# Carried states and decayed C of a chunked scan as 16-bit halves, and three steps in other places

## What is computed

```python
scores = jnp.einsum('bclhn,bcshn->bchls', Cc, Bc) * Lmat      # Lmat = exp of differences of cs, lower triangle
Ydiag = jnp.einsum('bchls,bcshp->bclhp', scores, xdt)         # xdt = x * dt
states = jnp.einsum('bclhn,bchl,bclhp->bchpn', Bc, decay_states, xdt)
def step(carry, inp):
    st, cd = inp
    return carry * cd[:, :, None, None] + st, carry
...
Yoff = jnp.einsum('bclhn,bchpn,bchl->bclhp', Cc, prev, jnp.exp(cs))
Y = (Ydiag + Yoff) + x * D
```

## Time and profile before

| | us |
|---|---|
| runs before: median of 3 (lowest to highest) | 2434.76 (2432.14 to 2435.37) |
| profiled execution, its own time | 2433.26 |
| its span, first to last instruction | 2431.4 |
| PE busy (share of span) | 2343.2 (96%) |
| DVE busy | 1794.1 (74%) |
| ACT busy | 1584.3 (65%) |
| POOL busy | 1377.3 (57%) |

### The profile page before, as it was taken

The page is one execution under the profiler, slowest core; times in us unless marked ns, Lnnn a source line. Parts: engine busy times, 40 slices in busy tenths (PEclk is TensorE's granted clock), DMA queues, the critical chain, the costliest instruction groups (busy, mean ns, idle before and its releaser), DMA issues. The chain is left out here.

```text
span 2431.4 us, 49850 instructions
## 1 busy us (share of the span) xinstructions
PE 2343.2 (96%) x16008; PEld 1328.4 (55%) x16008; DVE 1794.1 (74%) x3250; ACT 1584.3 (65%) x3327; POOL 1377.3 (57%) x1178
## 2 busy tenths in 40 slices
PE   6999999999999999999999998879999999999898
PEld 3555555555555555555555554445555556555444
DVE  6777777777777787777777885567787777888613
ACT  6776776776776776776776774355665555655533
POOL 5576576576576576576576579344344434454323
PEclk8999999999999999999999999889999999999999
DMA  7343343343343343343343441320010110100000
GB/s 244 120 134 113 111 136 113 112 137 111 111 137 111 110 136 113 112 137 111 112 137 110 132 152 36 129 89 14 36 40 14 41 36 14 40 10 14 1 1 35
DMA packets 117294, 218.95 MB, mean 90 GB/s; under 512 B 10016, under 2 KB 43424, under 8 KB 115840
## 3 DMA queue, kind: packets, MB, share of 16 engines
q1 hardware_dynamic: 116992, 215.29, 27.0%
HBM read 212.10 MB, written 3.15 MB: 89 GB/s over the span
## 5 line engine op out<-in xcount | busy, mean ns | idle before, releaser
L990 ACT ACTIVATE E<-wq,cst 128x128 f32<-128x128 f32 x1024 | 311.7, 389 | 2.2 <-PEq L298 2.2
L256 DVE SCALAR_TENSOR_TENSOR xc<-bank,taps,xc 128x511 f32<-128x511 f32 (+2 forms) x384 | 283.0, 737 | 24.6 <-ACT xc L243 24.1
L1963 POOL TENSOR_TENSOR qT<-qT,qrot 128x512 f32<-128x512 f32 x64 | 81.3, 1270 | 358.3 <-DVE qrot L1852 358.3
L1297 POOL TENSOR_TENSOR acc<-acc,sq 128x512 f32<-128x512 f32 x112 | 162.6, 1452 | 183.5 <-ACT sq L1002 183.5
L61 PE MATMUL bank<-xhi,wx 128*128 128x512 f16 x640 | 242.7, 379 | 0.0
L60 PE MATMUL bank<-xlo,wx 128*128 128x512 f16 x640 | 242.6, 379 | 0.0
L59 PE MATMUL bank<-xhi,wx 128*128 128x512 f16 x640 | 242.5, 379 | 0.0
L1109 DVE TENSOR_TENSOR E<-E,cbm 128x1024 f32<-128x1024 f32 x128 | 235.0, 1836 | 0.9
L1280 POOL TENSOR_TENSOR ecs<-ecs,xcC 128x768 f32<-128x768 f32 x128 | 235.2, 1837 | 0.4 <-POOLq L298 0.4
L1176 DVE SCALAR_TENSOR_TENSOR u<-xc,D,bank 128x512 f32<-128x512 f32 x128 | 95.7, 747 | 177.1 <-PE bank L815 166.4
L1285 POOL TENSOR_TENSOR xw<-xt,wdec 128x384 f32<-128x384 f32 x128 | 106.5, 832 | 174.5 <-DVE xt L1128 174.4
(11 more groups left out here) (265 smaller groups left out, 6617.3 us busy)
## 6 DMA issues: line engine op xcount, KB each, us to landing
wq<-cs_rows SPq DMA_DIRECT2D x128, 512.0 KB, 4.0
ecs<-ecs_rows SPq DMA_DIRECT2D x128, 384.0 KB, 3.6
wx<-in_w_xbc SPq DMA_DIRECT2D x80, 256.0 KB, 2.6
wz<-in_w_z SPq DMA_DIRECT2D x64, 256.0 KB, 2.6
wo<-in_w_o SPq DMA_DIRECT2D x64, 256.0 KB, 3.9
wq<-in_wq SPq DMA_DIRECT2D x8, 1024.0 KB, 5.6
awo_raw<-in_wo SPq DMA_DIRECT2D x32, 256.0 KB, 3.0
wkv<-in_wkv SPq DMA_DIRECT2D x8, 512.0 KB, 3.7
```

Source lines behind the costliest of these rows:

```text
L256: self.nc.vector.scalar_tensor_tensor(out=dst[:, d:T], in0=self.k.bank[bank][:, 0:T - d], scalar=self.taps[:, bass.ds(g, 1), b, j, 3 - d:4 ...
L990: ins = nc.scalar.activation(E[t.i % 4][:, h, c], sc.csr[t.i % 2][:, h, c * P:(c + 1) * P], ACT.Relu, scale=-1.0, bias=head(sc.cst, t, c, h))
L1297: nc.gpsimd.tensor_tensor(acc[t.b][:], acc[t.b][:], sq[:], ALU.add).then_inc(acc_done, 1)
```

## The change

- The carried states are kept once (`st`, no longer two buffers). ACT casts them to f16 (`sthi`, `leading_states`), DVE subtracts this from them into f16 (`stlo`, `rest_of_states`). POOL makes beside `ecs` a remainder `ecslo` of it in f16, once the scan of the tile before is done (y_ready), since there is one buffer.
- The scan's fp32 product of state and C becomes three 16-bit ones per head and chunk, on the same 64-column halves. The scan waits for `cs_lo` and `st_lo` instead of cs_done.
- On DVE `xt` goes behind the first tap, `ylo` behind the second. On POOL `decayed_x` goes ahead of the low halves of the z weights.
- `exps` of two tiles are written at the end of odd slots instead of at the head of even ones.

```diff
@@ buffers
-        st = [sb(f"st{i}", [P, CH - 1, P]) for i in range(2)]
+        st = sb("st", [P, CH - 1, P])
+        sthi, stlo = sb("sthi", [P, CH - 1, P], F16), sb("stlo", [P, CH - 1, P], F16)
...
+        ecslo = sb("ecslo", [P, 2, T - P], F16)
@@ PE, scan
-                    pe.wait_ge(cs_done, t.n + 1)
+                    pe.wait_ge(cs_lo, t.n + 1)
+                    pe.wait_ge(st_lo, t.n + 1)
...
-                        for h in range(2 if c else 0):
-                            r = slice(h * HD, (h + 1) * HD)
-                            mm = nc.tensor.matmul(Y[r, cols], st[t.i % 2][:, c - 1, r], sc.ecs[t.i % 4][:, h, (c - 1) * P:c * P],
-                                                  start=False, stop=True, skip_group_check=True)
+                        e, d = sc.ecs[t.i % 4], slice((c - 1) * P, c * P)
+                        for x in range(3 if c else 0):
+                            for h in range(2):
+                                r = slice(h * HD, (h + 1) * HD)
+                                mm = nc.tensor.matmul(Y[r, cols], (sthi, sthi, stlo)[x][:, c - 1, r],
+                                                      (lead(e[:, h, d]), ecslo[:, h, d], lead(e[:, h, d]))[x],
+                                                      start=False, stop=x == 2, skip_group_check=True)
@@ ACT
+                def leading_states(t):
+                    act.wait_ge(s_step, 3 * t.n + 3)
+                    nc.scalar.copy(sthi[:], st[:]).then_inc(st_hi, 1)
...
                 def slot(g, m):
                     s = tile_at(g, m)
-                    if m % 2 == 0:
+                    if isinstance(s.n, int) and s.n == 0:
                         for d in (1, 2):
-                            if tile_at(g, m + d):
-                                exps(tile_at(g, m + d))
+                            exps(tile_at(g, m + d))
                     square(s)
                     leading(s)
+                    if tile_at(g, m + 1):
+                        leading_states(tile_at(g, m + 1))
...
+                    if m % 2:
+                        for d in (2, 3):
+                            if tile_at(g, m + d):
+                                exps(tile_at(g, m + d))
                     if is_last_unit(s):
                         tail(s)
@@ DVE
+                def rest_of_states(t):
+                    dve.wait_ge(st_hi, t.n + 1)
+                    nc.vector.tensor_tensor(stlo[:], st[:], sthi[:], ALU.subtract).then_inc(st_lo, 1)
...
                         masked(n1)
+                        rest_of_states(n1)
...
-                        taps("x", sc.xc[n3.i % 4], n3, 2 + n3.i, (remainder, lambda: turned_x(n2)))
+                        taps("x", sc.xc[n3.i % 4], n3, 2 + n3.i, (lambda: turned_x(n2), remainder))
@@ POOL
                                             ALU.mult).then_inc(cs_done, 1)
+                    pool.wait_ge(cs_done, t.n + 1)
+                    wait(pool, y_ready, t.n)
+                    nc.gpsimd.tensor_tensor(ecslo[:], e[:], lead(e[:]), ALU.subtract).then_inc(cs_lo, 1)
...
-                        if 9 <= mm:
-                            sc.split_wz(pool, s.g + 1, mm - 9)
+                    if tile_at(g, m + 2):
+                        decayed_x(tile_at(g, m + 2))
+                    if more and 9 <= mm:
+                        sc.split_wz(pool, s.g + 1, mm - 9)
                     if m == 16:
                         sc.split_wz(pool, s.g, XT - 1)
-                    if tile_at(g, m + 2):
-                        decayed_x(tile_at(g, m + 2))
```

More of the change, by code:

```diff
@@ L667, in mixer @@
         cs_done, xw_done, acc_done, rstd_done = S("cs_done"), S("xw_done"), S("acc_done"), S("rstd_done")
+        st_hi, st_lo, cs_lo = S("st_hi"), S("st_lo"), S("cs_lo")
         acc_split, xw_lo, bt_done = S("acc_split"), S("xw_lo"), S("bt_done")
@@ L1019, in first @@
                     gate(tile_at(0, 0))
+                    leading_states(tile_at(0, 0))
                     decays(tile_at(0, 1))
@@ L1114, in state @@
                         dve.wait_ge(st_ready, t.n + 1)
-                        nc.vector.tensor_copy(st[t.i % 2][:, 0], W[:, 0:P]).then_inc(s_step, 1)
+                        nc.vector.tensor_copy(st[:, 0], W[:, 0:P]).then_inc(s_step, 1)
                         return
@@ L1120, in state @@
                         mm = nc.vector.scalar_tensor_tensor(
-                            out=st[t.i % 2][:, c, r], in0=st[t.i % 2][:, c - 1, r], scalar=head(sc.cd, t, c, h),
+                            out=st[:, c, r], in0=st[:, c - 1, r], scalar=head(sc.cd, t, c, h),
                             in1=W[:, c * P + h * HD:c * P + (h + 1) * HD], op0=ALU.mult, op1=ALU.add)
                     mm.then_inc(s_step, 1)
+                def rest_of_states(t):
+                    dve.wait_ge(st_hi, t.n + 1)
+                    nc.vector.tensor_tensor(stlo[:], st[:], sthi[:], ALU.subtract).then_inc(st_lo, 1)
                 def turned_x(t):
@@ L1168, in first @@
                     masked(tile_at(0, 0))
+                    rest_of_states(tile_at(0, 0))
                     turned_x(tile_at(0, 1))
```

## The result

The changed kernel takes **2478.6 us** (median of 4 runs, 2474.4 to 2480.1) against 2433.5 of the kernel before (2430.7 to 2435.4): a ratio of 1.0182, 95% interval 1.0170 to 1.0195. It is slower by 45 us; the forecast was 35.

What follows compares the result with a forecast made beforehand. PE bounds the loop, POOL the last unit. PE's part -15.7, stalls +41, late `xwlo` +7, former gate wait -6.6, last unit +8.8 sum to +34.5 us: 2469 us, range for 8 in 10 2426 to 2503.

Steps and rivals of the forecast that it cites:

- The bound and the direction: PE sets the loop's time, its wait for the gate's silu on ACT (6.6 us) is second; the change slower, chance 0.76.
- PE's part, -15.7: PE's state products in the scan: 0.173 us a chunk instead of 0.218, -15.7 us over the 120 tiles before the last unit.
- Rival 3: PE's 16-bit pairs in the scan go no faster than fp32 ones, 0.109 us a pair: 2514 us, chance 0.10.
- ACT's cast, 0.43 a slot: New cast `sthi` on ACT's way to the gate: 0.5 us less 0.07 of overlap, 0.43 in every slot.
- `stlo`, 0.47 and 0.8 of waiting: DVE's new subtraction ahead of the taps: 0.47 us, plus some 0.8 of waiting beside wx on POOL.
- `ecslo` beside u times the gate, 0.4: At the scan's end, POOL's `ecslo` starts as DVE reaches u times the gate and costs DVE 0.4 to 0.6 us.
- wz later helps: In POOL's queue, the low halves of wz behind `xw` and `xwlo` help keep the next states from waiting; no separate size.
- late `xwlo`: POOL's `xwlo` queues behind `ecslo` and the next states wait for it: 7 us, bounded by 0 and 16.
- D = 1.8: D is the lateness of ACT's silu: 1.8 us with DVE-POOL collisions, 1.0 without.
- The stalls: PE's waits for the gate: 2.03 us in slots 0 and 8, 0.72 in 6 and 14; 41 us over 7.5 passes.
- The last unit, +8.8: POOL sets the pace at the end; six `ecslo` of 1.47 us add 8.8 us, at most 10.9, least 0.
- Rivals 1 and 2: Rival 1: collisions do not add up, D = 1.0, 2439 us, 0.20; rival 2: DVE's new work hidden, 2425 us, 0.15.

## Why the prediction was right, and where it was not

- **The bound and the direction: right.** What was second in line, the gate on ACT, became first; 47.4 us of waiting for `gz` against the 41 forecast, more than PE gained.
- **PE's part, -15.7: right.** A chunk takes 784.33 - 784.16 = 0.17 us as forecast, and the scan up to the states 785.21 - 783.67 = 1.54 instead of 768.60 - 766.92 = 1.68: 0.14, 17 us over 120 tiles; the mean over these tiles is 0.125, 15 us. Rival 3 fell: a pair takes 0.06, not 0.109.
- **ACT's cast, 0.43 a slot: right.** 0.43 in four stalls a pass and 7.5 passes is 13; leaving it out gave 13.6.
- **`stlo`, 0.47 and 0.8 of waiting: near in size.** Mean 1.19 us, 1.11 less the overlap of 0.08. The partner is most often `acc` (41 of 128); the named wx is it in 21.
- **`ecslo` beside u times the gate, 0.4: near in the mean, by luck; the reason failed.** The product went from 0.82 to 1.17 us in the mean. The step rested on "POOL idle" at the scan's end. In the changed kernel POOL is not idle there: in slot 14 `ecs` itself ends at 787.85, 2.6 us behind the scan's end; it ended 0.14 ahead of it before (768.46). So the product met `ecs` in 60 of 128 tiles and took up to 2.34 us instead of 1.2, and without `ecslo` it still took 1.08 in the mean. Slots 10, 12 and 14 bear it, with 1.1 to 1.45 more each; slots 11, 13 and 15 have nothing.
- **The moved POOL step: wrong in sign.** "wz later helps" was one of the reasons for a small charge on the late `xwlo`. Beside the new work, the new order costs 12 us. The charge itself, +7, was nearly met (2.7 to 8.0: +5.3), and it is the early `xt` that keeps it there.
- **D = 1.8: too small where it mattered, since each slot's lateness was reckoned afresh.** Against the states the silu is 3.14 - 0.12 = 3.0 us later in slot 14 and as much in slot 6, but 1.9 in slot 8 and 1.3 in slot 0 of this pass. The 3.0 of slot 14 can be taken apart: 1.45 (1.67 - 0.22) is handed on from slot 12 by DVE, a term the forecast did not have; `stlo` gives 781.50 - 780.18 = 1.32 where 1.27 was forecast, `ylo` 0.13 where it was 0.15, u times the gate of slot 13 nothing where it was 0.4; and the states start 0.14 earlier.
- **The stalls, slot by slot: near in sum, wrong in distribution.** Summed over all passes, the idle time ahead of the scan rose behind slots 0, 6, 8 and 14 from 3.3, 0, 0 and 1.5 us to 9.3, 8.4, 9.8 and 11.4. The forecast had 15 each for slots 0 and 8 and 5 each for 6 and 14. Slot 1, not on the list, went from 3.6 to 8.0. That the sum came near is luck in part: two slots were put too high, two too low.
- **The last unit, +8.8: a little low.** The stretch from scan 120 to scan 127 grew by 10.5, near the upper end of 10.9. `ecslo` takes 1.47 where nothing stops it, as forecast, and leaving it out gave 7.4 back.
- **The sum.** In the profiled executions the way from scan 0 to scan 120 grew by 35.3 us, where -15.7 + 34.4 + 7 = 25.7 was forecast. What PE executed there fell by 12.3 us (15.7 forecast); its idle time ahead of the scan rose by 38.2 (34.4), that ahead of the states by 5.8 (7). Another 3.6 the forecast did not have: PE's wait for DVE's u ahead of the gate's projection, 0.4 before and 4.0 now. So no single term makes the error of 10 us; a lateness of DVE that lasts over slots is in the two largest, the idle time ahead of the scan and this wait. The last unit added 10.5 (8.8). Behind the last scan 4.1 us came back (918.2 us instead of 922.3) and 0.5 ahead of the first; no run looked for why. That makes 41.2, and the median of the four runs lies 4.2 above this execution.

Rivals 1 and 2 needed D at 1.0 and below 0.67; it was 1.3 to 3.0.

## What to carry to other kernels

Where DVE and POOL both work out of SBUF, cost an added elementwise instruction on either by its length plus that of what it can meet on the other, and look at all of POOL's queue and not at the new instruction alone: shifting an old one into DVE's way cost 12 us here, which came back when it stood again where POOL waits anyway. Before splitting work finer, see whether one operand of a colliding DVE instruction can stay in PSUM; that one edit gave back 28 us here, and only 3 in the kernel before, where PE hardly waited for the gate. And follow lateness over several slots: a slot's slack is spent by the slot before it.

## What was not expected of the hardware

- A DVE instruction with two SBUF operands that met one of POOL ended a fixed time behind the end of POOL's, whenever it had begun: `stlo` 0.41 or 0.42 us in all 91 cases of a wait, u times the gate 0.55 in all 91, the mask 1.08 or 1.09 in all 113. So DVE's price for a collision is about what POOL's instruction has left to run when DVE's begins.
- With one operand in PSUM, u times the gate did not change by more than 0.02 us in 128 cases, and writing u to PSUM instead of SBUF cost 0.01 us (751 ns against 741 in the mean).
- Three pairs of 16-bit matmuls with 64 columns each ran at 0.057 us a pair with weight loads of 0.11 us in the records, beside the matmuls. The Trainium skill (TensorEngine Tiling (Array Packing), section "Restrictions and Gotchas") has column tiling without the fast weight load; what the loads did cost, they did not hold the pairs up here.
